# Second attention of a two-layer block: who splits the head outputs, and in which unit maxima, outputs and weight copies stand

## Chip, cores and metric

The kernel runs on one core of one Trainium2 chip. The time is the device time of one execution in microseconds. Three executions of the kernel before took 1001.75, 999.77 and 999.84 us, median 999.84.

## The reference, cut to what matters

Two layers follow each other, each with an attention and a feed-forward part. Layer 0 attends from 2 x 1024 tokens to 77 context words and has a ternary feed-forward. Layer 1 attends to the tokens themselves and the words, and then sends each token to 2 of 8 experts beside a shared one. The change touches the attention of layer 1, here called the second attention:

```python
xn, ln = layernorm(ctx), layernorm(x)            # keys and values come from both
q = split_heads(ln @ Wq.T)                       # 4 heads of 64, 2 batches of 1024 tokens
k, v = split_heads(concat(xn @ Wkv.T, ln @ Wlkv.T))
attn = softmax(mask(rmsnorm(q) * scale @ rmsnorm(k).T))   # 1024 x (1024 + 77)
x = x + (attn @ v) @ Wo.T + bo
```

Beside it the expert weights are prepared for later: each is split into a high part (rounded to the format of the fast matrix product) and a low part (the rest), so that products keep nearly full precision.

## The kernel before

The second attention is a chain of 8 steps, numbered n = 0 to 7, each for one head of one batch (b alternates). Step 0 is written out, steps 1 to 6 are three passes of a hardware loop with two steps each, step 7 is written out. A step has NU = 18 units: 9 tiles of keys (8 of 128 tokens, one of 77 words) times 2 halves of 512 queries.

TensorE (`step` from L1026) issues in unit q, in this order: the two score products of unit q + 1 (`scores`, L987 and L988, banks 3 and 4 in turn), transposes of the next head (`turned`, L952, units 0 to 3), the value product of unit q (`values`, L995, two passes), a maxima product for the next head (`maxima`, L964, into banks 0 to 2, units 5 to 12) and an output product of the head before (`joined`, L1009 and L1010, into bank 7, also units 5 to 12, in the last step 4 to 11). Units 15 and 16 carry the turned maxima (`minus`, L977). In step 0 the next head's work comes three units later.

ACT takes each score bank through the exponential (L1518, L1520), which both the value product of that unit and the scores two units on wait for. Between exponentials it keeps the high parts of the next head's queries and keys (`high`, L1491), and copies the high part of an expert weight piece (`conv`, L1504) in the units of `CONV_AT` (in the last step of `CONV_END`), six per step. At the end of a step it empties the two value banks into `oT` (L1547, L1548). In the next step it makes two copies of it: `o_hi` (L1523, unit 1), the high part, and `o_x` rows 64 up (L1525, unit 2), the whole.

VectorE (`step` from L2004) makes the two low parts of the output (`outputs_low`, L1996: 64 rows into `o_x`, and one row of sums into `o_hi`) between the low parts of the next head's queries and keys (`low`, L1963; for the context words two more operations, L1969 and L1970, which release the first maxima product). Then it takes per token tile the maximum (L1977) and adds the output product to the tokens (L1986, L1988). At the end it scales queries and keys of the head after the next (`scaled`, L1944 twice, L1949), which the transposes of the next step wait for.

POOL per step: the values of a coming head (`head_values`, L609, L610), a copy of the next head's keys (`head_keys`, L613, once VectorE has them), then six low parts of weight pieces (`conv`, L640). Behind the second step of each loop pass it adds one part of a bias split (L657, L658 and, but for the last, L660).

SyncE waits for each low part, loads a raw piece into the slot just read (three slots) and stores the finished piece of 1 MB (L477) from one of three slots of `cv_hl`. ACT's copy number p waits until the store of p - 3 has landed and raw piece p has come. Behind the last store SyncE loads the shared expert (L411).

Behind step 7 the first half of the tokens is normalised, transposed (`tokens_T`, L1023) and split, and the last head's output is joined (`joined_last`).

## Time and profile before

| | |
|---|---|
| median of three runs | 999.84 us |
| profiled execution | 998.9 us |
| its span | 997.2 us |
| second attention, steps 0 to 7 | from about 224 to 528 us of the span |
| TensorE busy, of the span | 883.1 us, 89% |
| VectorE, ACT, POOL busy | 695.4, 535.1, 373.2 us |

The times of the rows below are microseconds from the start of the span, durations too unless marked ns. A row of the timeline has start, duration, engine, line, operation, output and inputs, the count of merged instructions, and in brackets the engine's idle time before it with what released it. The ends of matrix products are modelled, so their starts are the better measure. PEld is the loading of weights into TensorE.

### The profile page before, as it was taken

The numbers are of one execution on the slowest core, as the hardware profiler recorded it, in microseconds if no ns is written. First come the engines' busy times: TensorE is split into PE (matmuls) and PEld (weight loads), VectorE is DVE, ScalarE is ACT, GpSimd is POOL, SyncE is SP. The second block draws the span as 40 slices with busy tenths as digits, with TensorE's granted clock in tenths as the row PEclk, the third lists the DMA queues.
The fourth block names the chain that finished last, engine by engine and source line by source line (L and its number), as shares of the span: only waits on it lengthen the run. The fifth ranks groups of instructions, "written<-read, shape, count | busy, mean of one in ns | idle before, by whom it ended". The sixth has DMA issues, their size and how long they took to land.

```text
span 997.2 us, 15053 instructions
## 1 busy us (share of the span) xinstructions
PE 883.1 (89%) x4259; PEld 614.2 (62%) x4263; DVE 695.4 (70%) x1345; ACT 535.1 (54%) x848; POOL 373.2 (37%) x303
## 2 busy tenths in 40 slices
PE   8975678988999989989889899989999999999991
PEld 3643445544454444454447687677888888788881
DVE  4778987875676886876478677865666666565666
ACT  2436776436646746746743633424666666565650
POOL 1123332545263863854612454631222222222310
PEclk9998998999999999999998999999999999999995
DMA  9300000005575775774981500019660078617314
GB/s 304 86 1 1 0 0 1 1 0 193 198 285 185 290 269 197 291 264 172 355 317 49 232 1 1 1 47 416 218 247 32 32 296 314 265 37 278 95 35 169
DMA packets 49493, 153.96 MB, mean 154 GB/s; under 512 B 6176, under 2 KB 24024, under 8 KB 43822
## 3 DMA queue, kind: packets, MB, share of 16 engines
q1 hardware_dynamic: 45710, 144.17, 38.8%
q0 software_dynamic: 3744, 9.31, 2.9%
q8 instruction: 19, 0.31, 0.1%
q14 instruction: 20, 0.16, 0.0%
HBM read 97.89 MB, written 56.49 MB: 155 GB/s over the span
## 4 chain that ended last, share of the span: by engine, by line
PE 48%; DVE 20%; DMA 10%; issue 8%; ACT 7%; POOL 4%; SPq 1%; DVEq 0%; ACTq 0%; POOLq 0%
PE banks L995 7%; PE banks L1241 5%; PE banks L1243 5%; PE banks L1242 5%; DMA aux<-moe_x,small 5%; DMA wsplit<-cv_hl 4%; PE banks L964 2%; PE banks L987 2%; PE banks L905 2%; ACT wexp L1518 2%; PE banks L988 2%; POOL cv_hl L640 1%; DVE small L1849 1%; PE banks L1266 1%; PE banks L1268 1%
## 5 line engine op out<-in xcount | busy, mean ns | idle before, releaser
L995 PE MATMUL banks<-wexp 128*65 128x512 f32 (+1 forms) x288 | 151.1, 605 | 15.8 <-ACT wexp L1518 15.7
L640 POOL TENSOR_TENSOR cv_hl<-wexp,cv_hl 128x1024 fp32r<-128x1024 f32 x45 | 111.2, 2481 | 59.3 <-ACT cv_hl L1504 59.3
L1241 PE MATMUL banks<-ring,x_hi 128*128 x312 | 127.5, 409 | 0.0
L1243 PE MATMUL banks<-ring,x_lo 128*128 x312 | 122.1, 391 | 0.0
L1242 PE MATMUL banks<-ring,x_hi 128*128 x312 | 122.0, 391 | 0.0
L1518 ACT ACTIVATE wexp<-banks 128x512 f32<-128x512 f32 x128 | 75.4, 601 | 75.0 <-PE banks L988 74.8
L1977 DVE TENSOR_REDUCE small<-banks 128x1 f32<-128x1101 f32 x64 | 83.4, 1304 | 40.8 <-PE banks L964 40.8
L1651 ACT ACTIVATE banks<-wexp 128x1024 f32 x72 | 73.4, 1020 | 47.7 <-DVE aux L2343 47.7
L1634 ACT ACTIVATE aux<-banks 128x512 f32<-128x512 f32 x78 | 46.6, 597 | 63.0 <-PE banks L1243 47.1
L987 PE MATMUL banks<-q_hi,k_hl 128*128 128x512 f32 x144 | 75.4, 523 | 1.8 <-ACT q_lo L1495 1.0
L1243 PEld LDWEIGHTS banks<-ring,x_lo 128*128 128x128 f32 x312 | 58.5, 188 | 12.9
L2342 DVE TENSOR_TENSOR aux<-banks,aux 128x512 f32<-128x512 f32 x39 | 27.0, 692 | 56.1 <-ACT aux L1634 56.1
L2335 DVE TENSOR_TENSOR aux<-banks,aux 128x512 f32<-128x512 f32 x39 | 27.0, 692 | 55.4 <-ACT aux L1634 55.4
L1241 PEld LDWEIGHTS banks<-ring,x_hi 128*128 128x128 f32 x312 | 58.9, 189 | 9.9 <-issue 0.2
L1242 PEld LDWEIGHTS banks<-ring,x_hi 128*128 128x128 f32 x312 | 58.9, 189 | 9.6
L702 POOL DMA_INDIRECT moe_y<-aux,small x20 | 20.6, 1030 | 118.0 <-DVE aux L2353 118.0
L964 PEld LDWEIGHTS banks<-k_hl,q_hi 128*128 128x128 f32 x192 | 32.2, 189 | 52.1 <-DVE small L1977 32.0
L995 PEld LDWEIGHTS banks<-wexp 128*65 128x65 f32 (+1 forms) x288 | 36.7, 139 | 44.2 <-ACT wexp L1518 27.5
L1504 ACT ACTIVATE cv_hl<-wexp 128x1024 fp32r<-128x1024 f32 x45 | 51.5, 1144 | 22.0 <-DMA wsplit<-cv_hl 22.0
L1107 PE MATMUL banks<-xh,ring 128*128 128x512 f32 x128 | 52.1, 407 | 7.7 <-DVEq L2107 6.3
L964 PE MATMUL banks<-k_hl,q_hi 128*128 128x512 f32 (+1 forms) x192 | 52.3, 380 | 7.5 <-DVE k_hl L1970 6.1
L702 POOL DMA_INDIRECT moe_y<-small x19 | 19.3, 1016 | 102.8 <-DVE small L2353 102.8
(358 smaller groups left out, 2254.0 us busy)
## 6 DMA issues: line engine op xcount, KB each, us to landing
wsplit<-cv_hl SPq DMA_DIRECT2D x45, 1024.0 KB, 7.8
ring<-wsplit SPq DMA_DIRECT2D x32, 1280.0 KB
wexp<-in_L_ffn_w SPq DMA_DIRECT2D x40, 512.0 KB, 5.8
wexp<-in_expert_biases SPq DMA_DIRECT2D x8, 1152.0 KB, 6.7
ring<-wsplit SPq DMA_DIRECT2D x4, 1024.0 KB, 8.4
wexp<-moe_y SPq DMA_DIRECT2D x8, 512.0 KB, 6.4
wexp<-in_L_ffn_sw SPq DMA_DIRECT2D x5, 512.0 KB, 10.7
x_sb<-in_x SPq DMA_DIRECT2D x4, 512.0 KB, 7.4
```

The source lines that it names most:

```text
L640: g.tensor_tensor(sides(hl[:, PIECE:2 * PIECE]), raw, sides(hl[:, 0:PIECE]).bitcast(f32), ALU.subtract).then_inc(s['cv_lo'], 1)
L964: last = mm(banks[:, o + a:o + a + w], q_hi[b][:, t * P:(t + 1) * P], k_hl[b][:, a:a + w], start=True, stop=True)
L987: mm(pb[3 + q % 2][0:w, :], k_hl[b][:, a:a + w], q_hi[b][:, cols], start=True, stop=False)
L995: mm(pb[5 + half][0:DA, :], vh[b][0:w, c, :], pT[q % 3][0:w, :], start=c == 0, stop=c == len(KTILES) - 1).then_inc(s['a_pv'], 1)
L1107: mm(o[:], hi, xh[:, kc, tok], start=kc == 0, stop=False)
L1241: mm(o[:], x_hi[u][:, kc, :], hi, start=kc == 0 and not primed, stop=False, skip_group_check=primed)
L1242: mm(o[:], x_hi[u][:, kc, :], lo, start=False, stop=False, skip_group_check=primed)
L1243: last = mm(o[:], x_lo[u][:, kc, :], hi, start=False, stop=primed and kc == KC - 1, skip_group_check=primed)
L1504: a(sides(hl[:, 0:PIECE]), raw, ACT.Copy).then_inc(s['cv_hi'], 1)
L1518: a(pT[q % 3], pb[3 + q % 2][:], ACT.Exp).then_inc(s['a_p'], 1)
L1651: a(banks[:, 2 * side * 512:2 * side * 512 + 2 * I], of_bias(u, side * 2 * I, 2 * I), ACT.Copy).then_inc(m['up_bias'], 1)
L1977: v.tensor_reduce(mx8[:, t:t + 1], banks[:, o:o + S + SK], AX.X, ALU.max).then_inc(s['a_mx_free'], 1)
```

## The change

POOL takes over the two low parts of the head output from VectorE and the whole copy into `o_x` from ACT. In its step it now waits for `oT`, makes the values of a coming head, then the three output operations, then the first weight split, then the key copy, then five more splits. ACT makes `o_hi` in unit 0, right behind the first exponential, and its weight copies move from units 1, 4, 7, 9, 12, 14 to 3, 5, 7, 9, 11, 13 (last step: from 0, 2, 4 to 3, 5, 7). Maxima and output products move one unit later, from 5 to 12 to 6 to 13 (in step 0 the maxima stay). In the last step the output products stand two per unit in units 6 to 9. VectorE makes the negated maxima ahead of the last output tile. In the last step ACT copies the first half of the output one product earlier, and VectorE takes the output halves ahead of the third and fourth token splits.

```diff
-        CONV_AT = (1, 4, 7, 9, 12, 14)
-        CONV_END = (0, 2, 4)
+        CONV_AT = (3, 5, 7, 9, 11, 13)
+        CONV_END = (3, 5, 7)
@@ POOL
-            def head(n, h, b):
-                pool.wait_ge(s['a_o'], n - 1)
-                head_values(h, b)
-                pool.wait_ge(s['a_khl'], n + 1)
-                head_keys(b)
+            def outputs(n):
+                pool.wait_ge(s['a_o'], n + 1)
+                pool.wait_ge(s['a_ohi'], n + 1)
+                g.tensor_tensor(o_x[0:DH, :], oT[0:DH, :], o_hi[0:DH, :].bitcast(f32), ALU.subtract).then_inc(s['a_olo'], 1)
+                pool.wait_ge(s['a_v'], n + 3 if n < B * NH - 2 else n + 2)
+                pool.wait_ge(s['a_olo'], 2 * n + 1)
+                g.tensor_tensor(o_hi[DH + 32:DH + 33, :], oT[DH:DA, :], o_hi[DH:DA, :].bitcast(f32), ALU.subtract).then_inc(s['a_olo'], 1)
+                pool.wait_ge(s['a_olo'], 2 * n + 2)
+                g.tensor_copy(o_x[DH:P, :], oT[0:DH, :]).then_inc(s['a_odup'], 1)
+                pool.wait_ge(s['a_odup'], n + 1)
...
-                    head(i * 2 + (2 + b), i + 1, b)
+                    n = i * 2 + b
+                    pool.wait_ge(s['a_o'], n + 1)
+                    head_values(i + 1, b)
+                    outputs(n)
                     for p in range(PER_STEP):
-                        conv((i * 2 + b + 1) * PER_STEP + p)
+                        if p == 1:
+                            pool.wait_ge(s['a_khl'], n + 3)
+                            head_keys(b)
+                        conv((n + 1) * PER_STEP + p)
...
+            outputs(B * NH - 2)
             for p in range(PER_STEP * (B * NH - 1), CONV):
@@ TensorE
-                lag = 3 if first else 0
+                lag, head_at = (3, 5) if first else (0, 6)
...
+                    if 6 <= q < 6 + TB // 2 and last:
+                        joined(n - 1, h_last, out_at, 2 * (q - 6))
                     values(n, b, q)
...
-                    if 5 <= q - lag < 5 + TB and not last:
-                        maxima(n + 1, use, 1 - b, q - lag - 5)
-                    out_q = q - (4 if last else 5)
-                    if 0 <= out_q < TB and not first:
-                        joined(n - 1, h_last, out_at, out_q)
+                    if head_at <= q - lag < head_at + TB and not last:
+                        maxima(n + 1, use, 1 - b, q - lag - head_at)
+                    if 6 <= q < 6 + TB and not first and not last:
+                        joined(n - 1, h_last, out_at, q - 6)
+                    if 6 <= q < 6 + TB // 2 and last:
+                        joined(n - 1, h_last, out_at, 2 * (q - 6) + 1)
@@ ACT
-                    if q == 1 and not first:
+                    if q == 0 and not first:
                         act.wait_ge(s['a_o'], n)
                         a(o_hi[0:DA, :], oT[0:DA, :], ACT.Copy).then_inc(s['a_ohi'], 1)
-                    if q == 2 and not first:
-                        a(o_x[DH:P, :], oT[0:DH, :], ACT.Copy).then_inc(s['a_odup'], 1)
+                    if q == NU - 1 and last:
+                        outputs_hi(0, n)
...
                 if last:
-                    for half in range(2):
-                        a(o_hi[0:DA, half * 512:(half + 1) * 512], pb[5 + half][0:DA, :], ACT.Copy).then_inc(s['a_ohi'], 1)
...
+                    outputs_dup(0)
+                    outputs_hi(1, n)
+                    outputs_dup(1)
@@ VectorE
                     for k in range(5):
-                        if not first and k < 2:
-                            outputs_low(n - 1, k)
                         low(n + 1, 1 - b, k, use + 5)
-                elif last:
-                    for k in range(2):
-                        outputs_low(n - 1, k)
                 for t in range(TB):
                     if not last:
                         maximum(n + 1, t)
+                    if not last and t == TB - 1:
+                        minus(n + 1)
...
-            for p in range(3):
+            for p in range(2):
                 tokens_low(p)
             for half in range(2):
                 outputs_last(half)
-            tokens_low(3)
+                tokens_low(2 + half)
```

## Rows read from the trace of the kernel before

**Rows 1.** Windows, steps 1 to 6: stretch, length, busy engines, granted clock, DMA share, GB/s.

```profile
264.60:301.10 36.50, 34.34 (x137) 18.41 (x137) 25.86 (x37) 22.88 (x35) 16.75 (x9) 1.00 0.55 216
301.10:338.20 37.10, 34.80 (x138) 18.38 (x137) 26.59 (x37) 22.99 (x35) 18.73 (x10) 1.00 0.68 258
338.20:376.00 37.80, 34.46 (x138) 18.31 (x137) 30.40 (x38) 23.12 (x35) 25.90 (x12) 1.00 0.64 240
376.00:413.20 37.20, 34.76 (x138) 18.36 (x137) 26.52 (x37) 23.01 (x35) 18.71 (x10) 1.00 0.70 266
413.20:452.70 39.50, 36.06 (x138) 19.38 (x137) 30.46 (x38) 22.99 (x35) 26.25 (x12) 0.96 0.65 238
452.70:489.40 36.70, 34.41 (x138) 18.40 (x137) 21.17 (x34) 22.94 (x35) 18.34 (x10) 1.00 0.67 254
```

**Rows 2.** Waits of 227 to 525 us: who waited for whom, us, times, longest.

```profile
ACT cv_hl L1504 <- DMA wsplit<-cv_hl: 22.0, 8, 3.7
...
PE banks L995 <- ACT wexp L1518: 15.7, 24, 1.6
```

**Rows 3.** Timeline of TensorE in step 2.

```profile
301.13 0.49 PE L987 MATMUL banks<-q_hi,k_hl 128*128 128x512 f32 x1
...
304.40 1.02 PE L995 MATMUL banks<-wexp 128*65 128x512 f32 x2
...
306.56 1.07 PE L995 MATMUL banks<-wexp 128*65 128x512 f32 x2 [0.24 <-ACT wexp L1518]
...
324.89 1.07 PE L995 MATMUL banks<-wexp 128*65 128x512 f32 x2 [1.41 <-ACT wexp L1518]
...
327.07 1.02 PE L995 MATMUL banks<-wexp 128*65 128x512 f32 x2
...
331.41 1.02 PE L995 MATMUL banks<-wexp 128*65 128x512 f32 x2
...
332.74 1.02 PE L995 MATMUL banks<-wexp 128*65 128x512 f32 x2
```

**Rows 4.** Timeline of ACT in step 2.

```profile
303.33 1.07 ACT L1523 ACTIVATE o_hi<-wexp 65x1024 fp32r<-65x1024 f32 x1
...
304.85 1.17 ACT L1504 ACTIVATE cv_hl<-wexp 128x1024 fp32r<-128x1024 f32 x1
...
306.53 1.06 ACT L1525 ACTIVATE o_x<-wexp 64x1024 fp32r<-64x1024 f32 x1
...
323.23 1.12 ACT L1504 ACTIVATE cv_hl<-wexp 128x1024 fp32r<-128x1024 f32 x1 [3.44 <-DMA wsplit<-cv_hl]
```

**Rows 5.** Timeline of VectorE: one row of step 0, three of step 2, one of step 3.

```profile
242.03 1.50 DVE L1969 TENSOR_TENSOR k_hl<-k_hl,wexp 128x77 fp32r<-128x77 f32 x1
...
304.43 1.22 DVE L1996 TENSOR_TENSOR o_x<-wexp,o_hi 64x1024 fp32r<-64x1024 f32 x1 [3.78 <-ACT o_hi L1523]
...
312.53 0.24 DVE L1969 TENSOR_TENSOR k_hl<-k_hl,wexp 128x77 fp32r<-128x77 f32 x1
...
332.69 4.57 DVE L1944 TENSOR_TENSOR wexp<-wexp,small 128x1024 f32 x2
...
343.18 4.82 DVE L1996 TENSOR_TENSOR o_hi<-wexp,o_hi 1x1024 fp32r<-1x1024 f32 x1
```

**Rows 6.** Timeline of POOL in step 2 and at the start of step 3.

```profile
313.23 1.10 POOL L613 CAST k_hi<-k_hl 64x1101 fp32r<-64x1101 f32 x1 [9.89 <-DVEq L1973]
314.30 7.17 POOL L640 TENSOR_TENSOR cv_hl<-wexp,cv_hl 128x1024 fp32r<-128x1024 f32 x3
...
336.13 3.10 POOL L657 CAST wexp<-aux 96x2304 bf16<-96x2304 f32 x1
...
341.47 5.45 POOL L660 TENSOR_TENSOR aux<-aux,wexp 96x2304 f32<-96x2304 f32 x1
```

**Rows 7.** Timeline of TensorE at the end of step 7.

```profile
516.48 0.66 PE L1023 MATMUL banks<-ident,wexp 128*128 128x128 f32 x4 [1.75 <-DVE wexp L2071]
...
525.78 0.58 PE L1009 MATMUL banks<-wo,o_hi 97*128 97x258 f32 x1 [0.57 <-DVE xl L2077]
```

More of the change, by code:

```diff
@@ L1508, in tokens_hi, with outputs_hi, outputs_dup @@
                 a(xh[:, :, 2 * p * P:2 * (p + 1) * P], pb[XT_BANK[p]][:].rearrange("p (a b) -> p a b", a=KC), ACT.Copy).then_inc(s['r_xhi'], 1)
+            def outputs_hi(half, n):
+                act.wait_ge(s['a_pv'], n * NU + NU - 1 + half)
+                a(o_hi[0:DA, half * 512:(half + 1) * 512], pb[5 + half][0:DA, :], ACT.Copy).then_inc(s['a_ohi'], 1)
+            def outputs_dup(half):
+                at = slice(half * 512, (half + 1) * 512)
+                act.wait_ge(s['a_ohi'], HEADS + half)
+                a(o_x[DH:P, at], o_hi[0:DH, at].bitcast(f32), ACT.Copy).then_inc(s['a_odup'], 1)
             def step(n, b, use, first, last, turn, base):
@@ L1536, in step @@
                     minus(minus_at, 1 - b, 1)
-                act.wait_ge(s['a_pv'], n * NU + NU)
                 if last:
-                    for half in range(2):
-                        a(o_hi[0:DA, half * 512:(half + 1) * 512], pb[5 + half][0:DA, :], ACT.Copy).then_inc(s['a_ohi'], 1)
-                    for half in range(2):
-                        at = slice(half * 512, (half + 1) * 512)
-                        act.wait_ge(s['a_ohi'], HEADS + half)
-                        a(o_x[DH:P, at], o_hi[0:DH, at].bitcast(f32), ACT.Copy).then_inc(s['a_odup'], 1)
+                    outputs_dup(0)
+                    outputs_hi(1, n)
+                    outputs_dup(1)
                     act.sem_inc(s['a_o'], 1)
                 else:
+                    act.wait_ge(s['a_pv'], n * NU + NU)
                     a(oT[0:DA, 0:512], pb[5][0:DA, :], ACT.Copy)
@@ L2015, in step @@
                         maximum(n + 1, t)
+                    if not last and t == TB - 1:
+                        minus(n + 1)
                     if not first:
                         joined(use if last else use + 5, 1 - b, t, last)
-                if not last:
-                    minus(n + 1)
                 if more:
```

4 lines of the change are left out of this document (removed).

## The prediction

> **What bounds the kernel now.** I looked first at the parts of the page on time slices and costliest groups (TensorE nearly full through the second attention, its L995 the largest group), then at the table of windows with one window for each head step, the waits of the stretch, and the timelines of the engines. A step handles one head of one batch: 18 units, each with scores of the next unit, then values. Seven of the eight steps carry an older head's output as well. From the first score product of step 1 to that of step 7 is 36.5 + 37.1 + 37.8 + 37.2 + 39.5 + 36.7 = 224.8 us [rows 1]. TensorE is busy for most of it, but the waits show where it isn't: its value products (L995) waited 15.7 us for ACT's exponentials, and ACT's weight copies (L1504) waited 22.0 us for the stores of the slot they refill [rows 2].
>
> I take step 2 as the pattern and count from its start, S = 301.13; v is a unit's value product [rows 3]. What would it last if TensorE never waited? A plain unit is 332.74 - 331.41 = 1.33 us, one with a maxima product and an output product 327.07 - 324.89 = 2.18 us [rows 3]. From v10 (S+23.8) to the next step at 338.2 nothing stalls: 13.3 us [rows 1, 3]. Ahead of v10 lie three kinds of stall. v2 comes 2.16 us after v1 where a plain unit with four transposes takes 1.77 (estimate: plus 0.44), and v3 and v5 are late likewise, together 1.3 us: ACT did a weight copy (1.17) and then an output copy (1.06) between exponentials [rows 3, 4]. The first maxima product waits for VectorE, 0.4. And v10 is 1.6 late, because ACT stood 3.44 us before the copy at 323.23, whose slot was still being stored [rows 4]. Without these 3.3 us, and with one combined unit fewer ahead of v10 and one more behind it (2.18 - 1.33 = 0.85; the change puts the maxima into units 6 to 13), v10 is at S+19.6 and the end 14.2 later at S+33.8. Steps of 2.18 back and forth from v10 give v6 at S+10.9, v12 at S+24.0, v14 at S+28.3. Against 33.8 the six steps hold 224.8 - 202.8 = 22 us of stalls.
>
> **Part 1: ACT.** The 1.06 us output copy (L1525) leaves ACT, the other (L1523) goes ahead of the second exponential, and the first weight copy moves from unit 1 to unit 3. The copy began at 303.33, behind two exponentials of half a microsecond each; with it in the middle the second ends where the copy ended, near S+3.1 less ACT's overlap, and v1 starts at S+3.27 [rows 3, 4]. Each later exponential to v6 ends 0.1 to 0.5 us ahead of its need. So the early stalls go: about 1.3 us a step, cover thin but there.
>
> **Part 2: VectorE.** Its two subtractions of an output go, about 1.2 us each undisturbed and 4.82 where a POOL operation is under way [rows 5]. The chain to the last key part then ends by S+9.6. Its next operation, L1969, has two SBUF inputs: 0.24 us with POOL idle, 1.50 where a POOL subtraction ran [rows 5]. Now POOL's first weight split lies just there (S+8.7 to S+11.1), so L1969 ends near S+11.4 and the first maxima product can start at S+11.8. One unit later is S+11.7: the move by a unit is what pays for the lock, and cost is 0.1 us. If instead L1969 met a fresh split, it would be 1.1 us.
>
> The row shows the lock, 0.24 against 1.50 us. The Trainium skill ("SBUF — State Buffer", on the shared port pair) says the same: a VectorE instruction with two SBUF inputs and a GpSimd one that reads SBUF exclude each other for the whole instruction. "Perfetto Trace Analysis" in the Trainium skill goes further and warns that moving work between these two engines might not help; by that rule the outcome would be rival B below.
>
> **Part 3: POOL.** It gains two subtractions and a copy per step. Neither is in this trace on POOL. Nearest rows: three splits of 1024 columns in 7.17, so 2.4 us each, whatever the partitions; a cast of 1101 columns 1.10 [rows 6]. I take 2.4 + 2.4 + 1.0 = 5.9 us with gaps (bounds: 3.5 if narrow operands run as fast as VectorE's 1.22, 8.3 if one takes the 4.82 of a locked one [rows 5]). ACT's copy would end at S+2.5, so they end at S+8.6; the output product needs them at S+12.2 (v6, 0.9 for it and 0.5 for the maxima product). Hidden, 3.6 us to spare. The first split then runs to S+11.1 instead of S+15.5 (before: 314.30 + 2.4) [rows 6]. A slot came free 6.5 us after the end of its split (316.7 to 323.23) [rows 4, 6]: now S+17.6. ACT's fourth copy would have to start by S+17.9 for v10 not to wait. So the 1.6 us stall at v10 just goes. The key cast and the next two splits end at S+15.4 and S+17.8, their slots come free near S+22.3 and S+26.4 if the stores follow each other by 4.1 us; needed by S+22.2 and S+26.5. These margins are nothing, so I add 0.5 us a step (bounds 0 and 1.7): 34.3 us for each of steps 1, 2, 4 and 6.
>
> **Steps 3 and 5.** Behind the splits of steps 2 and 4 POOL does a bias part: a cast (3.10, but 1 us of it behind VectorE's scaling, which ended at 337.3: 2.1 by itself), a copy (the 2.1 up to 341.4) and a subtraction (5.45) [rows 5, 6]. Before, the sixth split ended about 2 us ahead of the next step, now some 4 us (S+30.0 of 34.3); but VectorE's scaled keys (two operations, 4.57 with POOL running [rows 5]) start at about S+29.8 and alternate with POOL's for the lock. Laid out: scaling to +31.2, cast to +33.3, scaling to +34.5, copy to +36.6, subtraction to +42.3, that is 8.0 us into the next step, where it was 341.47 + 5.45 - 338.2 = 8.7 [rows 1, 6]. Earlier POOL then had only a value copy ahead of its splits; now outputs stand there too: 8.0 + 0.9 + 5.9 = 14.9, and the output product wanted them at 12.2. TensorE waits 2.6 us. POOL's first split ends at 17.3, its slot is free at 23.8, and v10 follows 1.7 later at 25.5 instead of 19.6. From v10 a step has 14.2 us left, so it lasts 39.7; I take 39.8. If POOL wins the race at +29.8, the small scaling of the context keys ends up behind the 5.45 us subtraction, transposes wait 2.5 to 3.8 us, and outputs are no longer late: 38.4 to 39.6. So both orders make these steps about as slow or slower than their 37.8 and 39.5 now [rows 1].
>
> **Last step.** TensorE idles 1.75 us before the token transposes for the normalised tokens [rows 7]. Output products two per unit from unit 6 end two units earlier, so the VectorE chain behind them ends first and this goes. ACT's copies of the first half now overlap the last value product; the idle 0.57 us before the fourth output product goes too [rows 7]. Together 2.3 us. The weight stores of this step end 3 us later in it; the shared expert's loads behind them keep about 2 us of their margin (estimate from their issue after the last store).
>
> **Sum.** Four steps of 34.3 and two of 39.8 are 216.8; 224.8 - 216.8 = 8.0, plus 2.3 = 10.3 us. The profiled execution is 998.9 us in all (span 997.2), 0.9 under the median 999.84. 998.9 - 10.3 = 988.6; set against the median, 989.5. Step 0 has neither outputs nor slot waits of weight, I change nothing there. What follows the attention starts on its results and moves with it.
>
> **Rivals.** *A, cheap bias steps*: the lock falls so that steps 3 and 5 last 38, ordinary ones 33.8: 2 x 1.8 + 4 x 0.5 = 5.6 better, 984. For it: POOL finishes earlier within steps 2 and 4. Against: outputs still stand behind the bias part.
> *B, the gain goes back through port or slots*: L1969 meets a fresh split (1.1 us in six steps) or each slot comes 1 us later than I read. 6 x 1.1 = 6.6 worse: 996. For it: the margins of 0.1 us above. Against: L1969 starts 1 us behind the start of a split.
> *C, nothing is won*: the slot of v10 is the true limit and POOL's outputs only take the place of its wait for the keys. Outputs of 7.9 us a step would do it: 0 +- 2 us, 999.8.
> *D, slower*: POOL becomes the bound. Any time that its three operations take over 5.9 us goes straight to the first split, its store, ACT's fourth copy and v10. The decision point is 5.9 + 10.3 / 6 = 7.6 us. With one subtraction at 4.82 instead of 2.4 [rows 5] each of six steps pays 2.4: 14.4 - 10.3 = 4 us slower, 1004. For it: two waits for its own results stand between them. Against: at S+2.5 VectorE has only PSUM work, and three splits in a row went at 2.4 us each.
>
> **Chances.** Forecast (986 to 993.5) 0.58, A 0.14, B 0.15, C 0.07, D 0.06. TensorE's clock adds some: in step 5 the granted clock averages 0.96, a stretch at 1.2 instead of 2.4 GHz, where other steps show 1.00, and that step is 1.7 us longer than step 3 [rows 1]; the new stalls of 2.6 us may bring such a stretch in either step, or none, +-2 us. Range 982.5 to 996.5: it takes in A and B and leaves C and D out. About 0.2% (2 us) is what a measurement of this kernel can tell from none: faster 0.87 (forecast, A, B), same 0.07 (C), slower 0.06 (D).
>
> **What would show it.** Right: v2 within 1.8 us of v1; the copy of unit 9 with hardly a wait; ordinary steps of 34 to 34.5; idle time before the output product (L1009) in steps 3 and 5, released by POOL, 2 to 3 us; no idle time before the first token transpose. Wrong: POOL's new subtractions over 3 us; L1969 above 2 us; steps 3 and 5 under 38 or over 41; ordinary steps over 35.5, which would say the stores are the bound.

## The result, and the profile after

The changed kernel takes 989.39 us (median of 987.11 to 992.39; the kernel before beside it 1000.8), a ratio of 0.9884 with an interval of 0.985 to 0.992. The forecast was 989.5. The profiled execution took 988.14 us, its span 986.4. Among all executions below one was slow, 1002.05 us of the kernel with the last step's outputs one per unit: its median in the table includes it, its ratio doesn't.

First the windows of steps 1 to 7 in the trace after, which answer to [rows 1] (stretch, length, busy time of TensorE, its weight loads, VectorE, ACT and POOL, granted clock, DMA share, GB/s):

```profile
265.42:298.79 33.37, 33.37 (x137) 18.61 (x138) 22.79 (x35) 22.10 (x34) 22.09 (x12) 1.00 0.64 242
298.79:334.15 35.36, 34.18 (x139) 18.43 (x138) 24.37 (x34) 22.12 (x34) 26.15 (x14) 1.00 0.75 281
334.15:372.40 38.25, 35.51 (x139) 19.33 (x138) 30.53 (x37) 22.39 (x34) 28.39 (x14) 0.96 0.62 240
372.40:407.59 35.19, 34.16 (x139) 18.45 (x138) 24.37 (x34) 22.09 (x34) 25.99 (x14) 1.00 0.73 274
407.59:447.36 39.77, 35.70 (x139) 19.28 (x138) 30.14 (x37) 22.26 (x34) 28.55 (x14) 0.96 0.64 237
447.36:482.37 35.01, 33.85 (x138) 18.45 (x137) 20.87 (x32) 22.11 (x34) 25.82 (x14) 1.00 0.72 269
482.37:518.72 36.35, 32.33 (x121) 16.96 (x120) 21.67 (x70) 21.61 (x34) 13.73 (x9) 0.99 0.66 254
```

Steps 1 to 6 sum to 216.95 us where they were 224.8. Step 7, from its first score product to the first product of the shared expert, lasts 36.35 where it was 38.59. What follows is 467.7 instead of 469.1, and step 0 starts 0.7 later: both drift. Ordinary steps (1, 2, 4 and 6, those that don't follow a bias part) gained 2 us each, steps 3 and 5 nothing (78.0 us together, before 77.4).

The waits of the stretch from 227 to 515 us answer to [rows 2] (who waited for whom: us in total, times, longest). The renumbered lines: L1519 is ACT's weight copy, L1007 the value products, L1542 the exponentials, L964 the transposes of the next head (in the kernel before, L964 was the maxima), L1970 the scaling of the context keys.

```profile
ACT cv_hl L1519 <- DMA wsplit<-cv_hl: 35.8, 20, 3.4
...
PE banks L1007 <- ACT wexp L1542: 6.7, 6, 1.4
...
PE banks L964 <- DVE wexp L1970: 4.8, 2, 2.5
```

ACT waits longer for slots than before (35.8 against 22.0 us), yet the value products wait less (6.7 against 15.7): the slots come earlier, and most of what ACT waits lies beside TensorE's work. The third line is new, once each in steps 3 and 5.

Step 2 in the timelines of POOL, VectorE, ACT and TensorE (start, us, engine, line, operation; in brackets the idle time before it and its releaser). It starts at S = 298.79:

```profile
301.72 2.37 POOL L634 TENSOR_TENSOR o_x<-wexp,o_hi 64x1024 fp32r<-64x1024 f32 x1 [0.73 <-ACT o_hi L1547]
304.23 2.36 POOL L637 TENSOR_TENSOR o_hi<-wexp,o_hi 1x1024 fp32r<-1x1024 f32 x1
306.65 1.03 POOL L639 CAST o_x<-wexp 64x1024 fp32r<-64x1024 f32 x1
307.76 2.42 POOL L645 TENSOR_TENSOR cv_hl<-wexp,cv_hl 128x1024 fp32r<-128x1024 f32 x1
310.75 1.10 POOL L613 CAST k_hi<-k_hl 64x1101 fp32r<-64x1101 f32 x1 [0.56 <-DVEq L1994]
311.81 4.79 POOL L645 TENSOR_TENSOR cv_hl<-wexp,cv_hl 128x1024 fp32r<-128x1024 f32 x2
...
308.52 1.77 DVE L1990 TENSOR_TENSOR k_hl<-k_hl,wexp 128x77 fp32r<-128x77 f32 x1
...
316.84 1.16 ACT L1519 ACTIVATE cv_hl<-wexp 128x1024 fp32r<-128x1024 f32 x1 [1.72 <-DMA wsplit<-cv_hl]
322.67 1.12 ACT L1519 ACTIVATE cv_hl<-wexp 128x1024 fp32r<-128x1024 f32 x1 [3.20 <-DMA wsplit<-cv_hl]
...
324.33 1.07 PE L1007 MATMUL banks<-wexp 128*65 128x512 f32 x2 [1.18 <-ACT wexp L1542]
```

POOL's outputs end at S+8.9 (forecast 8.6), the first split follows them, and the key cast (L613) now stands between the first and the second split. The fourth weight copy (316.84) comes at S+18.05 (forecast 17.6), so v10 isn't late. The fifth comes at S+23.9 (forecast 22.3): v12 waits 1.18 us for it. That is why this step lasts 35.4 us and not 34.3. L1990, which was L1969, takes 1.77 us beside a split.

The start of step 3 (S = 334.15), VectorE, POOL and TensorE:

```profile
330.55 5.64 DVE L1965 TENSOR_TENSOR wexp<-wexp,small 128x1024 f32 x2
336.11 4.58 DVE L1970 TENSOR_SCALAR wexp<-aux,small 77x128 f32 x1
...
329.97 2.10 POOL L668 CAST wexp<-aux 96x2304 bf16<-96x2304 f32 x1
332.13 2.98 POOL L669 COPY bias_b<-wexp 32x2304 bf16<-32x2304 bf16 x1
335.19 5.42 POOL L671 TENSOR_TENSOR aux<-aux,wexp 96x2304 f32<-96x2304 f32 x1
...
340.75 1.11 PE L964 MATMUL banks<-ident,wexp 128*128 128x128 f32 x4 [2.35 <-DVE wexp L1970]
```

POOL's cast began 0.6 us ahead of VectorE's scaling. By their durations (the copy takes 2.98 us where it took 2.10 before) the two take turns from there, and the small L1970 ends up behind the 5.42 us subtraction; TensorE's transposes wait 2.35 us for it (2.50 in step 5).

### The profile page after: what moved, and what is told of

Read it like the earlier page. It is cut to its first block, busy times and chain, and to the rows that moved or that the text cites. A ratio compares the mean times of both kernels' runs of the same rounds, so it can differ in the third digit from the quotient of the medians.

```text
span 986.4 us, 15071 instructions
## 1 busy us (share of the span) xinstructions
PE 882.6 (89%) x4259; PEld 616.8 (63%) x4263; DVE 681.3 (69%) x1331; ACT 529.3 (54%) x841; POOL 408.6 (41%) x324
## 3 DMA queue, kind: packets, MB, share of 16 engines
q1 hardware_dynamic: 45710, 144.17, 39.2%
## 4 chain that ended last, share of the span: by engine, by line
PE 52%; DVE 21%; DMA 10%; issue 6%; ACT 5%; POOL 4%; SPq 1%; DVEq 0%; ACTq 0%; POOLq 0%
PE banks L1007 6%; PE banks L1256 6%; PE banks L1258 6%; PE banks L1257 6%; DMA wsplit<-cv_hl 4%; DMA aux<-moe_x,small 3%; PE banks L976 2%; PE banks L999 2%; PE banks L917 2%; PE banks L1000 2%; PE banks L1281 2%; POOL cv_hl L645 2%; PE banks L1283 1%; PE banks L1282 1%; DMA ring<-wsplit 1%
## 5 line engine op out<-in xcount | busy, mean ns | idle before, releaser
L1007 PE MATMUL banks<-wexp 128*65 128x512 f32 (+1 forms) x288 | 151.1, 606 | 6.8 <-ACT wexp L1542 6.7
L645 POOL TENSOR_TENSOR cv_hl<-wexp,cv_hl 128x1024 fp32r<-128x1024 f32 x45 | 108.5, 2419 | 45.3 <-ACT cv_hl L1519 44.8
L1542 ACT ACTIVATE wexp<-banks 128x512 f32<-128x512 f32 x128 | 76.1, 599 | 59.0 <-PE banks L1000 58.9
L1998 DVE TENSOR_REDUCE small<-banks 128x1 f32<-128x1101 f32 x64 | 83.5, 1304 | 34.8 <-PE banks L976 34.8
L999 PE MATMUL banks<-q_hi,k_hl 128*128 128x512 f32 x144 | 77.4, 537 | 1.7 <-ACT q_lo L1510 1.0
L1519 ACT ACTIVATE cv_hl<-wexp 128x1024 fp32r<-128x1024 f32 x45 | 51.2, 1137 | 35.8 <-DMA wsplit<-cv_hl 35.8
L976 PEld LDWEIGHTS banks<-k_hl,q_hi 128*128 128x128 f32 x192 | 31.7, 188 | 48.7 <-DVE small L1998 33.8
L1000 PE MATMUL banks<-q_lo,k_hi 65*128 65x512 f32 x144 | 57.6, 400 | 0.0
L1007 PEld LDWEIGHTS banks<-wexp 128*65 128x65 f32 (+1 forms) x288 | 37.8, 139 | 29.5 <-ACT wexp L1542 11.5
```

What stands on the lines that cost most here:

```text
L645: g.tensor_tensor(sides(hl[:, PIECE:2 * PIECE]), raw, sides(hl[:, 0:PIECE]).bitcast(f32), ALU.subtract).then_inc(s['cv_lo'], 1)
L976: last = mm(banks[:, o + a:o + a + w], q_hi[b][:, t * P:(t + 1) * P], k_hl[b][:, a:a + w], start=True, stop=True)
L999: mm(pb[3 + q % 2][0:w, :], k_hl[b][:, a:a + w], q_hi[b][:, cols], start=True, stop=False)
L1000: mm(pb[3 + q % 2][0:w, :], k_hi[b][0:DA, a:a + w], q_lo[b][0:DA, cols], start=False, stop=True)\
L1007: mm(pb[5 + half][0:DA, :], vh[b][0:w, c, :], pT[q % 3][0:w, :], start=c == 0, stop=c == len(KTILES) - 1).then_inc(s['a_pv'], 1)
L1542: a(pT[q % 3], pb[3 + q % 2][:], ACT.Exp).then_inc(s['a_p'], 1)
```

## Experiments

Outside the six steps a program's time drifts: in the profiles step 0 began between 223.2 and 236.1 us. So I judge the runs by the length of steps 1 to 6 in their traces, with the time and its ratio to the kernel before beside it. The kernel before took 999.66, 999.74 and 1001.6 us in the three groups of runs.

| kernel | steps 1, 2, 4, 6 | steps 3, 5 | sum | step 7 | time | ratio (interval) |
|---|---|---|---|---|---|---|
| before | 36.4, 37.1, 37.1, 36.7 | 37.8, 39.5 | 224.8 | 38.6 | 1000.8 | 1 |
| after | 33.4, 35.4, 35.2, 35.0 | 38.3, 39.8 | 216.9 | 36.4 | 989.4 | 0.988 (0.985-0.992) |
| after, again | 34.8, 35.0, 35.2, 35.0 | 38.2, 39.9 | 218.0 | 36.8 | 992.7 | 0.992 (0.989-0.995) |
| before, copies' units alone | 37.6, 36.9, 37.2, 35.8 | 38.3, 38.5 | 224.3 | 36.8 | 998.2 | 0.999 (0.995-1.003) |
| before, first split ahead of key cast alone | 34.8, 35.4, 35.4, 35.1 | 36.5, 38.1 | 215.4 | 37.8 | 990.0 | 0.990 (0.987-0.993) |
| after, copies' old units | 34.5, 34.9, 35.1, 34.7 | 38.6, 39.2 | 216.9 | 37.7 | 995.3 | 0.994 (0.991-0.998) |
| after, unit 5 | 34.7, 35.3, 35.3, 35.0 | 38.3, 41.2 | 219.8 | 37.0 | 994.2 | 0.993 (0.991-0.996) |
| after, outputs given back | 34.2, 34.7, 34.5, 35.3 | 36.7, 36.1 | 211.5 | 36.0 | 986.5 | 0.985 (0.979-0.991) |
| the same, key cast first | 38.0, 39.2, 36.9, 38.5 | 38.2, 39.8 | 230.6 | 36.3 | 1003.7 | 1.005 (1.002-1.008) |
| after, context keys first | 34.9, 35.3, 35.4, 35.1 | 39.9, 38.6 | 219.2 | 36.9 | 994.7 | 0.994 (0.991-0.997) |
| after, bias spread | 34.9, 35.9, 34.7, 35.9 | 35.5, 35.8 | 212.7 | 35.9 | 987.3 | 0.987 (0.981-0.993) |
| after, last step's outputs one per unit | 35.1, 40.6, 35.3, 35.1 | 35.8, 39.6 | 221.4 | 37.2 | 993.7 | 0.989 (0.985-0.993) |
| outputs given back, bias spread | 33.8, 34.4, 34.3, 35.0 | 33.9, 33.9 | 205.3 | 36.0 | 981.4 | 0.983 (0.979-0.986) |
| the same, copies 5 and 6 later | 34.4, 35.3, 35.3, 35.2 | 34.8, 34.8 | 209.7 | 35.9 | 984.0 | 0.983 (0.979-0.987) |

Between two traces of the changed kernel the sum differs by 1.1 us. Step 1 alone differs by 1.4: ACT's fifth copy found its slot at 21.8 us into the step in one trace and at 23.5 in the other, with the splits at the same places, so the stores land differently from run to run. The run with the last step's outputs one per unit has the code of the changed kernel in steps 1 to 6, so it is a third trace of them, with 221.4 us. In its step 2 the fifth copy found its slot only at 25.2 us, TensorE stalled for 2.48 us and ran at a lower clock behind that; POOL's bias cast and copy were then over before VectorE's scaling began, the bias subtraction ran beside the large scalings instead of ahead of the context keys, and step 3 lasted only 35.8. So a difference of less than 4.5 us between two sums shows nothing by itself, and what I read from such a difference rests on the waits beside it. Where a trace has a stretch of lower clock that the other hasn't, a step differs by up to 5 us: the run with the last step's outputs one per unit shows 40.6 at a granted clock of 0.92 in step 2.

**Bias operations spread.**

```diff
-                for k in range(PARTS)[i::NH - 1]:
...
+            BIAS_AT = {(2, 3): 0, (2, 4): 1, (3, 4): 2, (4, 3): 3, (4, 4): 4, (5, 4): 5, (6, 3): 6, (6, 4): 7}
...
                         conv((n + 1) * PER_STEP + p)
+                        if (n + 1, p) in BIAS_AT:
+                            pool.wait_ge(s['cv_lo'], (n + 1) * PER_STEP + p + 1)
+                            bias_op(BIAS_AT[n + 1, p])
```

> The changed kernel, with POOL's eight bias operations (three casts, three copies, two subtractions) no longer in one piece behind the splits of steps 2, 4 and 6: one or two of them follow the fourth and fifth split of each of steps 2 to 6, where POOL waited 1.3 to 3.7 us for ACT. My theory, that steps 3 and 5 are long (38.3 and 39.8 us against 35.0 to 35.4 in steps 2, 4 and 6) because the bias part meets VectorE's scaling and its 5.4 us subtraction holds back the context keys: the wait of TensorE's transposes for L1970 (2.3 and 2.5 us) goes, with it the drop of the granted clock to 0.96 in those steps, and both steps last 35.2 to 36. Time 989.4 - 7 = 982.5 (981.5 to 984). Rival, the long steps come from the clock alone, whose drop falls there for a reason of its own, or from the port being busy in total: both stay above 37.5 and the time is 987 or more.

Steps 3 and 5 fell to 35.5 and 35.8 at a clock of 1.00. The other four take 141.4 us together, against 138.9 and 140.0 in the two traces of the changed kernel: in all 212.7 us, somewhat over the 210 expected. The time, 987.3 us, missed the 981.5 to 984 that I gave. In step 3 nothing holds L1970 (here L1978) any more; VectorE's timeline:

```profile
335.84 2.35 DVE L1973 TENSOR_TENSOR wexp<-wexp,small 128x1024 f32 x2
338.11 0.28 DVE L1978 TENSOR_SCALAR wexp<-aux,small 77x128 f32 x1
```

So it is the bias part in one piece behind the splits that made steps 3 and 5 long; without its stall the clock didn't drop there either. The rival falls, since both steps are well under its 37.5 us, though the time is where it had put it (987 or more) and shows less of the gain than the trace.

**Context keys scaled first.**

```diff
-                for dst, a0, r0 in ((q_dup, 0, 0), (k_dup[:, 0:TB, :], D, NH)):
...
-                v.tensor_scalar(k_dup[0:SK, TB, :].rearrange("p (a d) -> p a d", a=2), csrc, rc, None, ALU.mult)\
-                    .then_inc(s['a_qk'], 1)
+                v.tensor_scalar(k_dup[0:SK, TB, :].rearrange("p (a d) -> p a d", a=2), csrc, rc, None, ALU.mult)
+                for name, dst, a0, r0 in (('a_q', q_dup, 0, 0), ('a_qk', k_dup[:, 0:TB, :], D, NH)):
...
+                    v.tensor_tensor(dst.rearrange("p t (a d) -> p t a d", a=2), src, r, ALU.mult).then_inc(s[name], 1)
```

> The changed kernel, with VectorE's scaling in another order: the context keys (L1970, 0.27 us undisturbed) first, then queries and keys, so that it can't end up behind POOL's 5.4 us bias subtraction. The bias part stays where it is. This makes the order that my forecast laid out first: no wait of the transposes in steps 3 and 5, and POOL's outputs late instead. If that layout holds (bias subtraction to 8.0 us into the step, outputs 0.9 + 5.9 behind it, wanted at 12.2), TensorE waits 2.6 us before the first output product and steps 3 and 5 stay at 38 to 39.8: time within 1.5 us of 989.4. Rival, the outputs come in time or less late since POOL's subtraction ran from 335.2 to 340.6 in the changed kernel and so ended 6.5 us into step 3: the wait is 1.1 us at most, the steps last 36 to 37.5 and the time is 985 to 987.

The transposes no longer wait, and step 3 is longer, 39.87 us, step 5 shorter, 38.58: together 78.5 against 78.0. The time was to be within 1.5 us of 989.4, and was 994.7. Its start (S = 346.24) in the timelines of POOL, VectorE and TensorE:

```profile
348.58 4.59 POOL L671 TENSOR_TENSOR aux<-aux,wexp 96x2304 f32<-96x2304 f32 x1
...
356.48 2.35 POOL L637 TENSOR_TENSOR o_hi<-wexp,o_hi 1x1024 fp32r<-1x1024 f32 x1
...
356.48 2.45 DVE L1988 SCALAR_TENSOR_TENSOR k_hl<-aux,k_hl 128x77 fp32r<-128x77 f32 x1
...
359.06 0.76 PE L976 MATMUL banks<-k_hl,q_hi 128*128 128x512 f32 x3 [0.96 <-DVE k_hl L1988]
360.38 0.38 PE L1021 MATMUL banks<-wo,o_hi 97*128 x1 [0.56 <-POOL o_x L639]
```

This is the order of my forecast: the subtraction ends at S+6.9 (forecast 8.0), outputs at S+13.7 (14.9), and both the maxima and the output product wait. The rival's 36 to 37.5 didn't come: TensorE waits 1.5 us there, but the first split starts at S+13.8, and the slots behind it are late as well. One of the two prices is paid in either order.

**The weight copies' units alone**, on the kernel before, and **the other way round**, on the changed kernel.

```diff
-        CONV_AT = (1, 4, 7, 9, 12, 14)
-        CONV_END = (0, 2, 4)
+        CONV_AT = (3, 5, 7, 9, 11, 13)
+        CONV_END = (3, 5, 7)
```

> The kernel before, with ACT's weight copies alone moved to the units that the change gives them (3, 5, 7, 9, 11, 13; in the last step 3, 5, 7). Outputs stay on VectorE and ACT, maxima and output products at unit 5. By my forecast the early stalls (1.3 us a step) go in part: the copy leaves unit 1, but ACT's output copy of 1.06 us stays in unit 2, so 0.8 us of it; and POOL's first split can start some 4 us earlier (behind the copy of unit 3), so the stall of 1.6 us ahead of v10 goes. Against it, this split now lies over VectorE's two subtractions (4.82 us instead of 1.22 for one that meets it) and over L1969. If the lock costs as little as I read, ordinary steps last 35 and the time is 1000.8 - 4 x 2 = 992 to 994. Rival, the subtractions on VectorE meet the earlier splits and hold up the key chain by 1.2 to 3.6 us in each of six steps: no gain or a loss, 999 to 1008. Then the copies' new places pay only together with the outputs on POOL.

224.3 against 224.8, and no measurable difference in time. The rival laid that to the subtractions on VectorE, but in step 2 they take 1.22 us each, undisturbed. What was in the way is POOL: its first split still stood behind the key cast, so it could not start 4 us earlier, as I had said. v6 came 1 us earlier (S+12.4 against 13.5), v10 still waited 1.51 us for its slot (before: 1.41), and the microsecond was lost again at the later slots. Step 2, POOL and ACT:

```profile
315.57 1.10 POOL L613 CAST k_hi<-k_hl 64x1101 fp32r<-64x1101 f32 x1 [8.84 <-DVEq L1973]
316.64 7.19 POOL L640 TENSOR_TENSOR cv_hl<-wexp,cv_hl 128x1024 fp32r<-128x1024 f32 x3
...
325.65 1.12 ACT L1504 ACTIVATE cv_hl<-wexp 128x1024 fp32r<-128x1024 f32 x1 [3.55 <-DMA wsplit<-cv_hl]
```

> The changed kernel, with ACT's weight copies in the units of before (1, 4, 7, 9, 12, 14; last step 0, 2, 4), all else as changed. By my forecast (part 1) the copy in unit 1 holds up the exponentials of units 1 to 4 by 1.3 us a step, less now that ACT's output copy is gone: 0.5 to 0.9. The first split starts no earlier (POOL is at the outputs until 8.7 us), so nothing comes back: 216.9 + 6 x 0.7 = 221 (219 to 223). Rival, the fifth and sixth copy, a unit later each, wait less for their slots (they wait 3.2 and 1.6 us in the changed kernel, and hold v12 up by 1.2): that gives back as much, 215 to 217.5.

216.9, the same sum as the changed kernel: the rival holds. In step 2 v6 starts at S+11.58 instead of S+10.98, so the early stalls of part 1 are there (0.6 us), but v12 starts at S+24.58 instead of S+25.54, since a copy that comes a unit later finds its slot. ACT's waits for slots are 11.8 us instead of 35.8, and those of the value products for exponentials 2.9 instead of 6.7. A new stall takes as much back: the turned maxima (L989) wait 3.8 us in six places for VectorE, which they did nowhere in the changed kernel. The last run of this section shows what that is. Step 7 is 37.7 us against 36.4 and 36.8.

**Outputs given back.** POOL's call goes, ACT copies behind the third exponential, VectorE subtracts ahead of its first two operations; all else stays.

```diff
-                    outputs(n)
...
+                    if q == 2 and not first:
+                        a(o_x[DH:P, :], oT[0:DH, :], ACT.Copy).then_inc(s['a_odup'], 1)
...
                     for k in range(5):
+                        if not first and k < 2:
+                            outputs_low(n - 1, k)
                         low(n + 1, 1 - b, k, use + 5)
```

> The changed kernel, with the outputs of a head given back: both subtractions to VectorE ahead of its first two operations of the next head, the copy to ACT behind the third exponential. Weight copies, maxima and output products stay where the change put them. By my account the outputs on POOL pay by what they take from VectorE (2 x 1.2 us and their meeting with splits) and ACT (1.06). Given back, POOL's first split runs at 6 to 8.5 us into the step, the next close behind, VectorE's second subtraction or L1990 meets one of them, and the first maxima product at 11.7 us waits 1 to 2 us: ordinary steps 36 to 37 instead of 35.2, steps 3 and 5 without output work behind the bias part about 37.5 instead of 39. Together 989.4 + 4 x 1.3 - 2 x 1.5 = 991.6 (989 to 995). Rival, the outputs' place is indifferent and the copies' places and the maxima's later unit hold the whole gain: 989 or less.

211.5 us: not slower but faster than the change, by 5.4 in the sum, and with 986.5 us where the rival had put it. The ordinary steps are the same within the repeat (138.7 against 138.9 and 140.0 us for the four). The gain is in steps 3 and 5, 72.8 against 78.0 and 78.1. It is seen best in step 3 against the second trace of the changed kernel, both at full clock (36.7 and 38.2 us). The fourth weight copy and v10, first with the outputs on POOL (S = 337.08), then given back (S = 338.92):

```profile
359.68 1.12 ACT L1519 ACTIVATE cv_hl<-wexp 128x1024 fp32r<-128x1024 f32 x1 [4.02 <-DMA wsplit<-cv_hl]
361.34 1.07 PE L1007 MATMUL banks<-wexp 128*65 128x512 f32 x2 [1.99 <-ACT wexp L1542]
```

```profile
358.37 1.13 ACT L1517 ACTIVATE cv_hl<-wexp 128x1024 fp32r<-128x1024 f32 x1 [0.62 <-DMA wsplit<-cv_hl]
```

S+22.6 against S+19.5: behind the bias part POOL has no outputs ahead of its first split, the slot is free 3 us earlier, and v10 (S+22.4 without a wait, S+24.3 with one) doesn't stall. In ordinary steps L1990 hardly meets a split, since ACT's first copy comes at S+7.1 and the split only behind it:

```profile
312.51 2.42 POOL L645 TENSOR_TENSOR cv_hl<-wexp,cv_hl 128x1024 fp32r<-128x1024 f32 x1 [6.09 <-ACT cv_hl L1517]
...
314.58 0.45 DVE L1990 TENSOR_TENSOR k_hl<-k_hl,wexp 128x77 fp32r<-128x77 f32 x1
```

POOL idled 6 us there. So in these traces the outputs on POOL bought nothing, and cost 5 us.

**Key cast ahead of the first split**, with the outputs given back, and **the first split ahead of the cast**, alone on the kernel before. The second is this edit; the first is its reverse:

```diff
             def head(n, h, b):
                 pool.wait_ge(s['a_o'], n - 1)
                 head_values(h, b)
-                pool.wait_ge(s['a_khl'], n + 1)
-                head_keys(b)
...
                     for p in range(PER_STEP):
+                        if p == 1:
+                            pool.wait_ge(s['a_khl'], i * 2 + b + 3)
+                            head_keys(b)
                         conv((i * 2 + b + 1) * PER_STEP + p)
```

> As the run with the outputs given back to VectorE and ACT (its steps 1 to 6 together 211.5 us), and besides POOL casts a head's keys ahead of its first weight split again, as in the kernel before, where the change has the split first. My theory from that run and from the one with the copies' places alone (224.3 us for the six steps against 224.8 before): what frees the slots is that the first split no longer waits for the key cast, and the copies' new units give nothing without it. Cast at 11.3 us into the step, so the first split ends at 14.8 instead of 10.7, its slot comes free at about 21, ACT's fourth copy and v10 are 2 to 2.5 us late: 211.5 + 6 x 1.7 = 221.7 (219 to 224). Rival, the later unit of maxima and output products carries the gain and the split's place little: 214 or less.

It took more than expected: 230.6 us, 19 more than with the split first and 6 more than the kernel before, part of it in clock (0.96 in four of six steps, one before); the rest of the 6 us wasn't followed up. Step 2 on POOL and ACT:

```profile
314.98 7.19 POOL L645 TENSOR_TENSOR cv_hl<-wexp,cv_hl 128x1024 fp32r<-128x1024 f32 x3
...
323.83 1.12 ACT L1516 ACTIVATE cv_hl<-wexp 128x1024 fp32r<-128x1024 f32 x1 [4.25 <-DMA wsplit<-cv_hl]
```

The fourth copy comes at S+21.0 as expected, and v10 at S+22.6.

> The kernel before, with one thing changed: POOL casts a head's keys behind its first weight split of the step and not ahead of it. Copies' units, outputs and maxima are those of before. My theory: this order is what frees the slot, since the cast waits until 12.1 us into the step for VectorE's key chain and the splits stood behind it (with the cast first the six steps took 230.6 us where 211.5 were taken otherwise). With ACT's first copy in unit 1 the split runs at 3.3 to 5.8 us and lies over VectorE's subtractions of the output, one of which takes 2.5 us more (as the 4.82 against 1.22 seen in step 3); the key chain and the first maxima product are 1 to 2 us later, and the wait of 1.6 us ahead of v10 goes, 2.5 us with what it costs behind. Together about 0.6 us less a step: 224.8 - 4 = 221 (218 to 223). Rival 1, the order alone carries the change's gain: 217 or less. Rival 2, the port takes all of it: 224 or more.

215.4 us, and a ratio of 0.990: rival 1 holds. One order on POOL, with nothing else touched, brings 9.4 us in the six steps, as much as the whole change. It brings 1.35 to 1.7 us in each of the six, which is the stall of 1.6 us ahead of v10; the value products wait 6.8 us for exponentials where they waited 15.7. The rest of the change takes 1.9 us off the four ordinary steps and adds 3.5 to steps 3 and 5. Step 2 (S = 301.77) on POOL, VectorE and TensorE:

```profile
306.74 2.41 POOL L638 TENSOR_TENSOR cv_hl<-wexp,cv_hl 128x1024 fp32r<-128x1024 f32 x1 [2.76 <-ACT cv_hl L1505]
313.87 1.10 POOL L613 CAST k_hi<-k_hl 64x1101 fp32r<-64x1101 f32 x1 [4.72 <-DVEq L1974]
...
306.98 3.25 DVE L1997 TENSOR_TENSOR o_hi<-wexp,o_hi 1x1024 fp32r<-1x1024 f32 x1
...
313.88 0.76 PE L965 MATMUL banks<-k_hl,q_hi 128*128 128x512 f32 x3 [0.17 <-DVE k_hl L1971]
```

The split ran at S+5.0 while POOL otherwise waited. It did lie over a subtraction (3.25 us instead of 1.22), but VectorE waited for ACT behind it anyway and the key chain ended at S+12.0, where it did before. My 1 to 2 us for this collision were wrong. The early stalls stayed (v2 at S+5.43, v6 at S+13.48), v10 came at S+22.2 where it was S+23.8, and nothing stalled behind it.

**Maxima and outputs at unit 5** on the changed kernel.

```diff
-                lag, head_at = (3, 5) if first else (0, 6)
+                lag, head_at = (3, 5) if first else (0, 5)
...
-                    if 6 <= q < 6 + TB and not first and not last:
-                        joined(n - 1, h_last, out_at, q - 6)
+                    if 5 <= q < 5 + TB and not first and not last:
+                        joined(n - 1, h_last, out_at, q - 5)
```

> The changed kernel, with maxima and output products at unit 5 again in steps 1 to 6. By my forecast the later unit pays for the lock: L1990 ran 1.77 us and the key chain ended about 11.6 us into an ordinary step, the first maxima product could start behind v5, at 10.3. It would wait 1.3 us, in each of six steps, and one combined unit more stands ahead of v10, whose slot is now there: 216.9 + 6 x 1.2 = 224 (221 to 226). Rival, the slots' waits come later in the step and take this up: what is lost at unit 5 is not waited for at v12, and the six steps stay within 2 us of 216.9.

219.8 us: 1.7 over the repeat of the changed kernel, of which step 5 with a clock of 0.92 has 1.3. The first maxima product waits as I had said,

```profile
314.89 0.76 PE L976 MATMUL banks<-k_hl,q_hi 128*128 128x512 f32 x3 [1.26 <-DVE k_hl L1991]
```

but ordinary steps last 35.25 and 35.26 where they last 35.36 and 35.19 in the changed kernel: v12, which waited 1.18 us there, doesn't wait here. The rival's mechanism holds, though the sum lies between the two bounds that I gave; that the clock in step 5 has nothing to do with it wasn't tested.

**The last step's output products one per unit**, from unit 4 as before.

```diff
-                    if 6 <= q < 6 + TB // 2 and last:
-                        joined(n - 1, h_last, out_at, 2 * (q - 6))
...
-                    if 6 <= q < 6 + TB // 2 and last:
-                        joined(n - 1, h_last, out_at, 2 * (q - 6) + 1)
+                    if 4 <= q < 4 + TB and last:
+                        joined(n - 1, h_last, out_at, q - 4)
```

> The changed kernel, with the output products of the last step one per unit from unit 4, as before, and not two per unit from unit 6. By my forecast the pairs let the VectorE chain behind them end two units earlier and remove the 1.75 us ahead of the token transposes: of the last step's gain of 2.3 us (38.59 to 36.35 in the trace of the change) this takes 1.0 to 1.8 back, and with outputs on POOL the first product at unit 4 (7.0 us into the step) waits for POOL's outputs that end at 8.7, another 1 to 1.7: last step 38.5 to 39.5, steps 1 to 6 unchanged at 216.9. Rival, the gain came from ACT's copies of the last output's first half beside the last value product: last step 37 or less.

The idle time before the token transposes is back to the hundredth, and the first output product waits for POOL:

```profile
498.26 0.36 PE L1021 MATMUL banks<-wo,o_hi 97*128 97x258 f32 x1 [0.64 <-POOL o_x L639]
...
515.43 0.66 PE L1035 MATMUL banks<-ident,wexp 128*128 128x128 f32 x4 [1.75 <-DVE wexp L2080]
```

Step 7 is 37.2 us against 36.4 and 36.8 in the two traces of the change: of the stalls of 2.4 us only 0.4 to 0.8 reached its end. Behind it products wait for VectorE in this run and in the changed kernel alike (1.53 us before the fourth output product of the last head). Neither bound that I gave was met.

**The changed kernel again, and the version that beats both.** The first edit of this section and the giving back of the outputs, put together:

> Outputs given back to VectorE and ACT, and POOL's bias operations spread between the fourth and fifth splits of steps 2 to 6. Both alone took time off the six steps of the changed kernel (216.9 us): 211.5 and 212.7. If they act on different stalls (the outputs on the slots and on L1990 in every step, the bias part on the transposes of steps 3 and 5), all six steps last 34.4: 206.5 us (205 to 208.5), time 980 (977 to 983). Rival, both work on POOL's load alone, so that one has taken what the other could: 210.5 to 212 and 985 to 988.

205.3 us, six steps of 34.2 on average, where my forecast for a step without a bias part was 34.3. All ran at full clock; windows of steps 2 to 4:

```profile
299.04:333.39 34.35, 34.10 (x139) 18.47 (x138) 24.05 (x37) 23.41 (x35) 20.53 (x11) 1.00 0.75 284
333.39:367.33 33.94, 33.74 (x139) 18.53 (x138) 25.17 (x36) 23.24 (x35) 20.93 (x10) 1.00 0.70 260
367.33:401.66 34.33, 34.06 (x138) 18.46 (x138) 24.97 (x39) 23.34 (x35) 20.52 (x11) 1.00 0.78 291
```

TensorE is idle for 0.2 to 0.3 us of each. Their gains add up (5.4 + 4.2 = 9.6 by themselves, 11.6 together), as they should where two edits act on different stalls. The time, 981.4 us, has a ratio to the kernel before of 0.983 (0.979 to 0.986) against 0.988 (0.985 to 0.992) for the change.

> The changed kernel itself once more, on the same chip and beside the run that follows, for how well the sum of steps 1 to 6 repeats (216.9 us in its trace) and for the difference in time to the version with outputs given back and bias operations spread. 216 to 218 in the trace, steps 3 and 5 again 38 to 40; time 987 to 991.

992.7 us, over the 991 that I gave, and 218.0 in the trace, with steps 3 and 5 at 38.2 and 39.9: the pattern repeats. Step 3 had a clock of 1.00 this time and was no shorter.

> Outputs given back to VectorE and ACT, bias operations spread (205.3 us for the six steps, time 981.4), and besides ACT's fifth and sixth weight copy one unit later (12 and 14 in place of 11 and 13). They waited 0.4 and 0.7 us for their slots there, in all 14.6 us over 20 copies. If these waits still hold up v12 and v14, the six steps fall to 203 to 204.5 and the time to 980; if they lie beside other work, it stays within 0.7 us of 205.3. Against the changed kernel on the same chip, 7 to 10 us faster.

```diff
-        CONV_AT = (3, 5, 7, 9, 11, 13)
+        CONV_AT = (3, 5, 7, 9, 12, 14)
```

209.7 us, 4.4 more than with units 11 and 13. The time, 984.0 us, has the same ratio of 0.983 and doesn't tell the two apart; it is 8.7 us less than the changed kernel beside it. The trace says where the 4.4 us are. Step 2 on POOL and VectorE, and the wait from 225 to 508 us:

```profile
326.63 2.41 POOL L645 TENSOR_TENSOR cv_hl<-wexp,cv_hl 128x1024 fp32r<-128x1024 f32 x1
...
327.26 1.81 DVE L2010 TENSOR_SCALAR small<-small 128x8 bf16<-128x8 f32 x1
...
PE banks L995 <- DVE x_sb L2017: 4.8, 6, 1.0
```

With the sixth copy in unit 14 POOL's last split runs just when VectorE negates the maxima (L2010), an operation that took 0.33 us in step 2 of the run before. It takes 1.81 here, VectorE's next ones are late, and the turned maxima (L995) wait for them 4.8 us in six places, against 0.6 in one.

## Why the prediction was right, and where it wasn't

- *Slots.* Right in mechanism. An earlier first split takes the stall ahead of v10 away (S+18.05 for the fourth copy, forecast 17.6; v10 at S+19.9, forecast 19.6). The cause is another than the one that I put first: not what moved between the engines, but that the split no longer stands behind the key cast. In the timeline of before it is plain to see: POOL waited 9.89 us at the cast [rows 6], and all three splits were queued behind it. I timed the new order in part 3 without pricing that swap by itself. Alone it is worth 9.4 us.
- *Part 1, copies two units apart.* The stalls of units 1 to 5 went as said, but with the copies' old units the sum is the same 216.9. I counted a gain ahead of v10 and not what a copy a unit earlier meets at the fifth slot, nor that the sixth in its old unit puts a split on the negated maxima.
- *Part 2, one unit later.* L1990 took 1.77 us and ended at S+11.5, as laid out (S+11.4), and the cost was nothing. "What pays for the lock" was wrong: at unit 5 the wait of 1.26 us is there and is made up at v12.
- *Part 3, outputs on POOL.* The duration was right: 2.37 + 2.36 + 1.03 us, ending at S+8.9, hidden in ordinary steps. As a gain it fell: with the outputs given back ordinary steps are no longer than with them on POOL, and steps 3 and 5 are 5.2 us shorter.
- *Ordinary steps.* 34.3 forecast, 33.4 to 35.4 measured, together 138.9 against 137.2. The mis-sized term is when the second slot comes free: I had it at S+22.3, 4.7 us behind the first, and it came at S+23.9, 5.8 behind, so that ACT waited 3.20 us and v12 1.18. Step 1 of the first trace, where it came at S+21.8, lasted 33.4.
- *Steps 3 and 5.* 79.6 forecast, 78.0 measured. But the sum went by the branch in which outputs come late, and in the trace no output product waited for POOL. POOL won the race, which I had as the other branch: transposes waited 2.35 and 2.50 us (forecast 2.5 to 3.8), and the steps took 38.25 and 39.77 (38.4 to 39.6). The first branch, made by an edit, gave 39.9 and 38.6 for the 39.7, with 1.5 us of waits in step 3 for the 2.6. That both branches cost about the same is what saved the sum.
- *Last step.* 2.3 forecast, 2.24 measured. But 38.59 was a trace with a clock of 0.95; with the copies' units alone the last step came to 36.8, and giving back the single output products cost 0.4 to 0.8. Of the two waits that were to go, the 1.75 us went, but the 0.57 before the fourth output product grew to 1.53, while one that I hadn't counted, 1.88 us before the first, fell to 0.58. So the agreement is partly luck.
- *The sum.* 216.8 against 216.9 is two errors of about 1.7 us that cancel. The repeat's 218.0 says how much such an agreement is worth.
- *The signs.* Met: v2 1.8 us behind v1, POOL's subtractions under 3 us, no idle time before the token transposes. Not met: the copy of unit 9 waited 1.72 us and not hardly at all (though v10 wasn't held up), ordinary steps of 35.0 to 35.4 in three of four, and no output product waited for POOL in steps 3 and 5.
- *The rivals.* The Trainium skill's warning ("Perfetto Trace Analysis", on optimizing Scalar/DVE operations), that shifting work between VectorE and GpSimd might not help, stood behind rival B and had 0.15. For the outputs taken by themselves it holds here: no gain in ordinary steps. That the whole change gained in spite of it comes mostly from the order on POOL.

## What to carry over

When an engine's queue has a step that waits long for another engine, look at what stands behind it that could go first: putting one instruction ahead of another on POOL took 9.4 us off the six steps here, where the whole change took 7.9 and its three moved operations bought nothing. A change in several parts that lands on its forecast hasn't shown that each part works; undo each one by itself, and the version that leaves out what doesn't pay is faster. Long operations on POOL belong beside VectorE's work on PSUM (the maxima of L1998 kept their 1.30 us beside a split of 2.42), one at a time, and not in a row ahead of something that is waited for. And when a copy moves by a unit, look at what the split behind it now lies on.

## What the hardware showed

- Where VectorE and POOL both have operations on SBUF queued, the durations fit an exchange in which they take turns, whole operations at a time: an operation of 0.28 us (L1970, one SBUF input) took 4.58 beside the bias subtraction, POOL's copy of 2.10 took 2.98, a scalar_tensor_tensor of 128x77 took 2.45 beside POOL's output subtraction where it takes 0.30, and an operation on 128x8 numbers (L2010) took 1.81 beside a split where it takes 0.33. In both traces of the changed kernel POOL's cast began 0.6 us ahead of VectorE's scaling (329.97 and 330.55 in the first), and the order came out alike.
- A slot's store doesn't land at a fixed distance. In step 2 of the changed kernel the fourth copy found its slot 6.7 us after the end of the split (316.84 - 310.18), the fifth 8.5 us (322.67 - 314.2, the end of the second split by half of 4.79). In step 1 of two traces of the same kernel the fifth differed by 1.7 us, and in step 2 of a third trace it came at S+25.2 instead of S+23.9. What decides it wasn't tested.
- Stalls of 2 us or more on TensorE are often followed by a lower granted clock, and not always: step 3 with its wait of 2.4 us had 0.96 in one trace of the same kernel and 1.00 in the other, at 38.25 and 38.16 us.
